# A fused SSM, layernorm and quantised-FFN kernel: its first step gets an order and PSUM slots of its own, weight preparation moves between engines and steps, and the B product runs in row tiles of 64

## The reference, cut to what matters

```python
x = L0_attn_x                                   # [4, 1024, 256]
xn = layernorm(x)                               # no gain, eps 1e-5
# block 1: state-space block
xz = xn @ W_in.T;  x_inner, z = split(xz)       # 512 + 512 columns
x_conv = silu(causal_depthwise_conv(x_inner, conv_w, 4 taps) + conv_b)
s_C = (x_conv @ W_x.T)[..., 16:32];  B = exp(B_log)
h[t] = 0.95 * h[t-1] + x_conv[t]                # scan over the sequence
y = h * (s_C @ B.T) * silu(z)
y = y @ W_out.T
ssm = layernorm(xn + y) * ln_g + ln_b
# block 2: quantised linear layer
xd, wd = dequant(mx_quantise(xn)), dequant(mx_quantise(weight))   # blocks of 32, fp6 grid
ffn = xd @ wd.T + bias
return x + ssm + ffn
```

## Time and profile before

| | |
|---|---|
| median of 3 runs | 261.01 us |
| the profiled execution | 259.93 us |
| span in its profile | 258.0 us |
| PE (TensorE) busy | 214.8 us, 83% |
| DVE (VectorE) busy | 226.9 us, 88% |
| ACT (ScalarE) busy | 154.3 us, 60% |
| POOL (GpSimd) busy | 201.9 us, 78% |
| mean granted TensorE clock | 0.973 |

### The profile page before, as it was taken

How to read it: one execution, slowest core, us unless ns; L and a number is a source line. 1 busy time by engine, 2 the same in 40 slices (tenths; PEclk the granted TensorE clock), 3 DMA queues, 4 the chain that set the end, 5 groups by cost and what they waited for, 6 DMA issues and landing times.

```text
span 258.0 us, 3473 instructions
## 1 busy us (share of the span) xinstructions
PE 214.8 (83%) x1252; PEld 177.1 (69%) x1252; DVE 226.9 (88%) x311; ACT 154.3 (60%) x234; POOL 201.9 (78%) x130
## 2 busy tenths in 40 slices
PE   0469974777699999987999978979999989979591
PEld 0348743346579895876898853868898958959491
DVE  3899999998596989959899999958999999996465
ACT  2786492456974265784896627675995644494310
POOL 1327948999994869999949699999689798996523
PEclk9999999799989999999999997999999999999989
DMA  7955000000000000000520200000020200000233
GB/s 233 298 194 161 1 3 0 0 1 0 0 0 3 1 3 0 0 0 4 163 81 3 81 0 1 3 0 0 3 81 1 83 1 0 3 0 0 83 111 135
DMA packets 10809, 11.18 MB, mean 43 GB/s; under 512 B 680, under 2 KB 10152, under 8 KB 10792
## 3 DMA queue, kind: packets, MB, share of 16 engines
q1 hardware_dynamic: 9520, 9.96, 11.7%
q10 hardware_dynamic: 1272, 0.99, 1.4%
HBM read 6.76 MB, written 4.19 MB: 42 GB/s over the span
## 4 chain that ended last, share of the span: by engine, by line
DVE 33%; POOL 31%; ACT 11%; issue 10%; PE 10%; DMA 4%; POOLq 0%; ACTq 0%; DVEq 0%
POOL hy L420 9%; DVE hy L1139 7%; POOL rstd L400 6%; POOL xc L412 6%; DVE xc L1110 6%; DVE fx L1177 3%; DVE rs L1167 2%; DMA y<-fx 2%; ACT rs L718 2%; ACT xn L625 2%; DVE bn L1047 2%; DVE fx L1169 2%; POOL rs L469 2%; DVE y_lo L1157 2%; ACT y_hi L694 2%
## 5 line engine op out<-in xcount | busy, mean ns | idle before, releaser
L807 PE MATMUL slot<-xn_hi,w_in_lo 128*128 128x512 f32 x128 | 53.5, 418 | 7.2 <-DVE xn_lo L1099 2.8
L412 POOL TENSOR_TENSOR xc<-xc,tap 128x1021 f32<-128x1021 f32 x16 | 46.0, 2880 | 15.4 <-DVE xc L1110 15.4
L808 PE MATMUL slot<-xn_lo,w_in_hi 128*128 128x512 f32 x128 | 52.1, 407 | 0.0
L809 PE MATMUL slot<-xn_hi,w_in_hi 128*128 128x512 f32 x128 | 52.0, 406 | 0.0
L1139 DVE TENSOR_TENSOR_SCAN hy<-decay,xc 128x1024 f32<-128x1024 f32 x16 | 46.4, 2907 | 0.2 <-ACT xc L677 0.2
L420 POOL TENSOR_TENSOR hy<-hy,sz 128x1024 f32<-128x1024 f32 x14 | 43.3, 3094 | 2.3 <-ACT sz L672 2.3
L1110 DVE SCALAR_TENSOR_TENSOR xc<-slot,cw,xc 128x1023 f32<-128x1023 f32 (+1 forms) x32 | 40.2, 1264 | 1.9 <-ACT tap L662 1.4
L807 PEld LDWEIGHTS slot<-xn_hi,w_in_lo 128*128 128x128 f32 x128 | 25.0, 196 | 18.3 <-DVE xn_lo L1099 3.6
L677 ACT ACTIVATE xc<-xc 128x1024 f32<-128x1024 f32 x16 | 17.0, 1060 | 27.8 <-POOL xc L412 27.8
L809 PEld LDWEIGHTS slot<-xn_hi,w_in_hi 128*128 128x128 f32 x128 | 25.0, 195 | 6.3
L808 PEld LDWEIGHTS slot<-xn_lo,w_in_hi 128*128 128x128 f32 x128 | 25.0, 196 | 5.1
(11 more groups left out here) (125 smaller groups left out, 574.9 us busy)
## 6 DMA issues: line engine op xcount, KB each, us to landing
x_in<-L_attn_x SPq DMA_DIRECT2D x3, 1024.0 KB, 5.6
y<-fx SPq DMA_DIRECT2D x6, 512.0 KB, 3.0
x_in<-L_attn_x SPq DMA_DIRECT2D x2, 512.0 KB, 4.1
rs<-L_attn_W_in SPq DMA_DIRECT2D x2, 512.0 KB, 8.6
y<-x_in SPq DMA_DIRECT2D x3, 256.0 KB, 3.3
...
```

The lines of the kernel that those rows point to most:

```text
L412: pool.tensor_tensor(xc[:, c, TAPS - 1:], xc[:, c, TAPS - 1:], tap0[:, c % 2, 0:n], ALU.add).then_inc(conv_ready, 1)
L807: pe.matmul(dst, w_lo, m_hi, start=first, stop=False)
L808: pe.matmul(dst, w_hi, m_lo, start=False, stop=False)
L809: return pe.matmul(dst, w_hi, m_hi, start=False, stop=last)
```

## The change

1. The first step (batch 0, step -1) has a list of its own, `first_step`, on each engine, and VectorE has a second list, `second_step(0, 1)`, for step 0. In the first list the low part of xn comes ahead of the FFN weight. `scale_ffn_weight` stays in the first step; `round_ffn_weight`, `dequantise_ffn_weight`, `w_ffn_low` and `sum_w_out` are now in step 0, with `w_ffn_transposes` (TensorE) and `w_ffn_high` (ScalarE).
2. TensorE makes 48 transposes of the identity ahead of the first `t_norm`, and 12 after the second. Batch 0 uses slots in another order (`FIRST_SLOT_*`), and `x_half(c = 0)` of every batch waits for the low part by halves.
3. GpSimd makes both parts of W_in (`split_w_in`); before, ScalarE made the high and VectorE the low one.
4. `ln_b` and `ffn_b` are loaded to two partitions each of a cleared tile; two GpSimd instructions replace six on them. The factor for g is folded into `inverse_deviation`.
5. B is kept whole, as `b_hi` and `b_lo`; the masks are gone. `s_product` sums chunks in pairs, so that s fills [128, 512], with the two halves of the sequence in the two halves of the partitions; `s_high` and `s_low` handle 512 elements and not 1024; `cb_product` contracts over 64 rows, the sequence halves in the two row halves of the array. It still has 4 products of 512 columns for each chunk.
6. SyncE waits for W_in ahead of issuing W_out, and for `wd_ready` ahead of x of batch 2, since scratch of the FFN weight now lies in `x_in[:, 2]`.

```diff
         SLOT_X = [1, 2, 0, 2]
         SLOT_Z = [1, 1, 1, 2]
+        FIRST_SLOT_X = [2, 0, 1, 0]
+        FIRST_SLOT_Z = [2, 1, 2, 1]
+        FIRST_SLOT_CB = [0, 2, 1, 0]
...
+            sp.wait_ge(w_in_loaded[1], 16)
             sp.dma_start(w_out_f, w_out.rearrange("(c p) o -> p c o", p=P)).then_inc(w_out_loaded, 16)
             for b in range(1, XS):
+                if b == 2:
+                    sp.wait_ge(wd_ready, 1)
                 sp.dma_start(x_in[:, b, :, :], x_tiles(b, 0, NT)).then_inc(x_loaded, 16)
...
+            def split_w_in(h):
+                cols = slice(h * DI, (h + 1) * DI)
+                pool.wait_ge(w_in_loaded[h], 16)
+                pool.tensor_copy(w_in_hi[:, :, cols], w_in_f[:, :, cols]).then_inc(w_in_hi_ready, 1)
+                pool.wait_ge(w_in_hi_ready, h + 1)
+                pool.tensor_tensor(w_in_lo[:, :, cols], w_in_f[:, :, cols], w_in_hi[:, :, cols].bitcast(F32),
+                                   ALU.subtract).then_inc(w_in_lo_ready, 1)
...
-            def mask_b():
-                act.wait_ge(mask_ready, 1)
-                act.wait_ge(b_lo_ready, 1)
-                act.activation(b_exp_lo, b_exp_lo, ACT.Copy, scale=b_mask[:, 1:2]).then_inc(b_masked, 1)
-                act.activation(b_exp, b_t[:, :].bitcast(F32), ACT.Copy, scale=b_mask[:, 0:1]).then_inc(b_masked, 1)
...
-                act.activation(s_hi[:, :], slot[SLOT_S][:, :], ACT.Copy).then_inc(s_hi_ready, 1)
+                act.activation(s_hi[:, :], slot[SLOT_S][:, 0:HALF], ACT.Copy, scale=row_sign[:, 0:1]).then_inc(s_hi_ready, 1)
...
-                for g in range(2):
-                    pe.matmul(slot[SLOT_CB[c]][:, half(g)], b_t[:, c * P:(c + 1) * P], s_lo[:, half(g)], start=True, stop=False)
-                    mm = pe.matmul(slot[SLOT_CB[c]][:, half(g)], b_t[:, c * P:(c + 1) * P], s_hi[:, half(g)],
-                                   start=False, stop=True)
+                for w in (b_lo, b_hi):
+                    for g in range(2):
+                        mm = pe.matmul(slot_cb(b, c)[:, half(g)], w[rows(g), c * P:(c + 1) * P], s_rows[rows(g), :],
+                                       start=w is b_lo, stop=w is b_hi)
...
+            def first_step(nxt):
+                pe.wait_ge(ident_ready, 2)
+                warm_up(48)
+                t_norm(nxt, 0)
+                t_norm(nxt, 1)
+                warm_up(12)
+                x_half(nxt, 0)
...
-                slot_free(nxt, (y_ready, NCH * here + 2, here))
+                slot_free(nxt, (y_ready, NCH * here + (3 if first(here) else 2), here))
                 t_norm(nxt, 1)
...
                 t_deq(here, 1)
+                if first(here):
+                    w_ffn_transposes()
                 slot_free(nxt, (xd_lo_ready, 2 * here + 1, here))
                 x_half(nxt, 1)
-                if first(nxt):
-                    w_ffn_transposes()
...
-                dve.tensor_tensor(s_lo[:, :], slot[SLOT_S][:, :], s_hi[:, :].bitcast(F32),
-                                  ALU.subtract).then_inc(s_lo_ready, 1)
+                dve.scalar_tensor_tensor(s_rows[:, :], slot[SLOT_S][:, 0:HALF], row_kind[:, 1:2], s_hi[:, :].bitcast(F32),
+                                         ALU.mult, ALU.add).then_inc(s_rows_ready, 1)
...
+                s_low(here)
+                y_product(here, 0)
+                scan(here, 3)
+                y_product(here, 1)
+                round_ffn_weight()
+                y_product(here, 2)
+                sum_w_out()
+                xn_low(nxt, 0)
+                dequantise_ffn_weight()
+                xn_low(nxt, 1)
+                block_max(nxt, 0)
+                y_product(here, 3)
+                xd_low(here, 0)
```

255 lines of the change are left out of this document (163 added, 92 removed).

## The result

The changed kernel takes **272.83 us** (median of 4 runs, 272.46 to 273.02); the kernel before, run beside it on the same chip, 260.41 (4 runs). The ratio is 1.046, with a 95% interval of 1.041 to 1.051: it is slower by 12.4 us. The forecast was 267.0 with a range of 257.5 to 270.5: right in sign, too small by 5.8 us, and outside the range.

The account below looks back on a forecast made before the run. The prediction saw a relay between VectorE and GpSimd, taking turns, as the bound. The profiled 259.93 us plus 7.2 at the first tile (first-step lead included), 0 elsewhere, gave 267.1, forecast as 267.0; range 257.5 to 270.5.

Parts of the forecast that it names:

- The stretch of the weights: Step 0, scan of chunk 3 to xn_low(1, 1): eight weight instructions take turns with GpSimd; 19.15 us, 8.6 waiting.
- What waits behind it: Step 0, behind xn_low(1, 1): TensorE comes last, at the lower clock; first tile at 86.7 against 79.53, +7.2 us.
- The steady steps: All steps: the B product gives 0, bounds -2.4 and +2 for the four steps; the loads give 0.
- The first step and its lead: First step: x ready at 17.6, -4.5 us; gate 1 leads by 4.3 us, scan of chunk 3 ends at 53.3.
- the weights slip through: Rival, step 0: the eight weight instructions do not wait; first tile at 76.4, -3.1, 256.8 us; chance 0.17.
- The warming misses: Rival, first step: clock stays low, transposes delay t_norm 3 us, lead under 1; about 271; chance 0.06, shared with more waiting.

Follow-up runs that it names:

- run 1: Changed kernel with the eight FFN weight instructions back in the first step, their low part, sum, transposes and high part following: 262.92 us, 1.010 of before.
- run 3: Changed kernel with each of the eight weight instructions split into two of half the columns, the same work in sixteen: 279.23 us, 1.070 of before.
- run 5: Kernel before with only the FFN weight's preparation and the sum of W_out moved late, into step 0: 273.58 us, 1.050 of before.
- run 4: Kernel before with the B product part alone (whole B in two parts, s in row halves, no masks): 259.01 us, 0.994 of before.
- Run 12: Kernel with weights early and lead refilled, plus chunk 2's taps ahead of chunk 0's silu, its convolution earlier, block maxima later: 258.26 us, 0.994 of before.
- run 6: Changed kernel without the 48 and the 12 warming transposes: 272.71 us, 1.048 of before.
- Run 11: Changed kernel with the scan of chunk 2 ahead of block 1's statistics on VectorE: 273.49 us, 1.053 of before.
- run 7: Changed kernel with weights early in the first step, plus the scan of chunk 3 ahead of y_product(0, 0): 262.60 us, 1.007 of before.

## Why the prediction was right, and where it was wrong

**The stretch of the weights: right.** From the end of the scan of chunk 3 to the end of `xn_low(1, 1)` I had 19.15 us, 8.6 of them waiting; it is 77.29 - 58.60 = 18.7, with 8.15 waiting. GpSimd idles 4.41 us ahead of `centre_w_out` (forecast some 4), L1279 to L1282 have 1.81 to 2.72 (forecast 1 to 2.8). The sum is better than its parts, though. I had 2.3 us of waiting on L1274, behind gate 3, and the rest of `round` free: gate 3 ran from 58.68 to 61.02, beside `y_product(1)` and the cast, so the cast took 1.67 (forecast 1.1) and L1274 its own 0.69; L1280 took 2.43 where I had 0.9. One turn less and one more made up for each other, and that is luck. That the weights wait, and for what, is not: runs 1, 3 and 5 show the mechanism from three sides. The Trainium skill, "SBUF — State Buffer", in its section "SBUF: two separate sides", says that of a VectorE instruction with two inputs in SBUF and a GpSimd instruction that reads SBUF, whichever starts first holds the shared port pair for the whole instruction and the other one blocks; these rows agree, down to the 0.55 us by which each of the four ends behind GpSimd.

**What waits behind it: right.** From that low part to the first tile I had 14.25 us; it is 91.06 - 77.29 = 13.8, with TensorE at 0.50 when the product starts.

**The steady steps: right at 0** for the B product and the loads; the gates of chunk 1 of batches 1 and 2 are 55.9 us apart in both kernels, and run 4 gains nothing past the first step.

**The first step and its lead: wrong, and this is the term that was mis-sized.** The step of the prediction is "brings gate 1 to its end at 45.6 ... a lead of 4.3 us ... and the scan of chunk 3 ends at about 53.3". The gate did end at 45.28. But the scan ended at 58.60, 5.3 us later than forecast and 1.8 later than before: where the sum held 3.5 us of lead, the run had a delay of 1.8.

Most of the lead was gone ahead of the first gate. At the first `taps` it was 3.0 us (19.16 for 22.16; forecast 4.5), at the first convolution 2.7 (21.83 for 24.53), and at the end of the first gate 0.5 (37.05 for 37.59; forecast 2.7, at 34.9). Rows of before (VectorE, GpSimd) and of the changed kernel (GpSimd):

```profile
24.53 2.60 DVE L1110 SCALAR_TENSOR_TENSOR xc<-slot,cw,xc 128x1023 f32<-128x1023 f32 x2 [0.30 <-ACT tap L662]
...
35.18 2.41 POOL L420 TENSOR_TENSOR hy<-hy,sz 128x1024 f32<-128x1024 f32 x1 [2.29 <-ACT sz L672]
...
34.66 2.39 POOL L437 TENSOR_TENSOR hy<-hy,sz 128x1024 f32<-128x1024 f32 x1 [5.66 <-DVE hy L1197]
```

From the convolution on, the lead went since the changed list has the convolution of chunk 2 ahead of the first scan, and VectorE waits 2.86 us for its tap; the list before had it behind that scan. Run 12 takes most of that wait away. My working had this wait too (`taps` of chunk 2 at 27.7), but let the first convolution start at 19.9, with x and VectorE ready together. It was 21.83: `xn_low` ended 1.1 us later than forecast, and `scale_ffn_weight` took 3.16 us and not 2.25, two of its instructions (0.67 for 0.17, 1.45 for 0.69) beside GpSimd's split of W_in, which I had taken as hidden. That x itself came at 19.16 and not at 17.6 cost at most 0.4 us (runs 6 and 11).

That gate 1 ended on time all the same is luck: gate 0 was 2.1 us late, and the scan of chunk 2, 2.2 us, which in my working, as in the kernel before, lay ahead of gate 1, lay behind it in the run. What I had taken to be a lead at gate 1 was mostly a change of order. Run 11 puts the scan back, and the gate moves while the scan of chunk 3 and the time stay.

What stands between gate 1 and the end of the scan of chunk 3 I had passed over in one sentence ("`quantise`, gate 2 and `s_low` follow"), with 7.7 us for it. It was 6.9 before and is 13.3 now. The 6.4 more are, from the rows: 4.4 up to the start of `quantise`, since the scan of chunk 2 and the statistics behind it now lie behind the gate; 1.3 in `quantise`, which waits for gate 2 (2.88 for 1.61); and 0.8 from there on, since `y_product(0)`, with a wait of 0.88 for the C product, now stands ahead of the scan.

**The end: 1.2 us that the forecast had no term for.** At the first tile I was short by 4.4 us: 5.3 for the scan, less 0.45 in the weights' stretch and 0.45 behind it. In step 2 come 1.2 more. TensorE of the changed kernel:

```profile
186.50:191.50 5.00, 5.00 (x23) 0.68 0.01 3
```

It is the same dip as in run 7, at the same place in the step, and the kernel before has it 20 us earlier in the step. That the step is longer when the dip stands there holds in all 13 traces (run 7); what places it the runs do not tell, and I leave that open. 4.4 + 1.2 and 0.2 of roundings are the 5.8 between 267.0 and 272.8.

Of the rivals, that the weights slip through was refuted at this place, and held one step earlier (run 1). "The warming misses" was half right: the clock fell, but the 48 transposes held nothing up, and there was no price to it. Its 271 is nearer to the 272.8 than the forecast is, but for another reason.
